# A softmax constant moved from the score products into ScalarE's exponentials, and the first chunk's output projection moved into the last attention group

## The reference, cut to what matters

```python
x = x + attention(layernorm(x))        # x: 2 batches x 1024 rows x 256
x = x + ffn(layernorm(x))
# attention: 32 query heads of width 8, 8 key heads
scores = einsum('bhqd,bhkd->bhqk', q, k) / sqrt(8)
amask = where((j >= i - 128) & (j < i), -1e10, 0)     # band below the diagonal
out = softmax(scores + amask) @ v ; out @ wo
# ffn: 2 shared experts on all rows, and 8 routed experts of which each row takes 2
# (sigmoid router), inner width 640, silu(gate) * up, then down
```

## Time and profile before

| | |
|---|---|
| median of 3 runs | 952.74 us (952.62 to 954.16) |
| the profiled execution | 952.9 us, span 951.2 us |
| mean granted clock of TensorE | 0.983 |
| busy share PE / DVE / ACT / POOL | 94% / 47% / 61% / 29% |
| chain that ended last | PE 78%, ACT 8%, DVE 6%, issue 5% |

### The profile page before, as it was taken

The page is one execution under the profiler, slowest core; times in us unless marked ns, Lnnn a source line. Parts: engine busy times, 40 slices in busy tenths (PEclk is TensorE's granted clock), DMA queues, the critical chain, the costliest instruction groups (busy, mean ns, idle before and its releaser), DMA issues.

```text
span 951.2 us, 24249 instructions
## 1 busy us (share of the span) xinstructions
PE 896.4 (94%) x8221; PEld 570.8 (60%) x8222; DVE 444.9 (47%) x761; ACT 583.4 (61%) x733; POOL 278.7 (29%) x422
## 2 busy tenths in 40 slices
PE   9959999999999999999988999999999999999994
PEld 6513333333333333333346888888887888888883
DVE  7724433444444334444456777656653433434332
ACT  4769999999999999999972423332222222222221
POOL 4403333233233333333330000000012545445442
PEclk9969999999999999999997999999999999999998
DMA  5433445555544455532202207100027864564521
GB/s 178 130 112 103 162 157 206 206 199 196 175 149 159 154 206 206 204 93 90 55 22 66 67 18 238 45 1 23 1 81 256 265 209 98 156 180 127 150 35 22
DMA packets 41951, 123.67 MB, mean 130 GB/s; under 512 B 7608, under 2 KB 22968, under 8 KB 35760
## 3 DMA queue, kind: packets, MB, share of 16 engines
q1 hardware_dynamic: 31152, 110.35, 34.0%
q0 software_dynamic: 7008, 9.70, 5.7%
q10 hardware_dynamic: 3744, 3.02, 1.0%
HBM read 74.03 MB, written 49.02 MB: 129 GB/s over the span
## 4 chain that ended last, share of the span: by engine, by line
PE 78%; ACT 8%; DVE 6%; issue 5%; SPq 1%; DMA 1%; DVEq 0%; POOLq 0%; POOL 0%; ACTq 0%
PE ps L1663 18%; PE ps L1811 14%; PE ps L1616 13%; PE ps L1765 11%; ACT arena L930 7%; PE ps L1830 7%; PE ps L1778 5%; DVE ps L1149 3%; PE ps L1557 2%; PE ps L1821 2%; PE ps L1716 1%; PE ps L1542 1%; PE ps L1792 1%; PE ps L1752 1%; PE ps L1734 1%
## 5 line engine op out<-in xcount | busy, mean ns | idle before, releaser
L930 ACT ACTIVATE arena<-ps 128x1024 f32<-128x1024 f32 x336 | 317.0, 1044 | 6.9 <-PE ps L1616 6.9
L1663 PE MATMUL ps<-arena 128*32 128x256 f32 x4096 | 265.1, 385 | 0.1
L759 POOL TENSOR_SCALAR_AFFINE_SELECT arena<-arena 128x512 f32<-128x512 f32 x240 | 150.0, 638 | 302.3 <-ACT arena L941 203.1
L1616 PE MATMUL ps<-arena 64*128 64x512 bf16 (+1 forms) x1280 | 184.5, 343 | 21.5 <-SPq L545 7.7
L1663 PEld LDWEIGHTS ps<-arena 128*32 128x32 f32 x4096 | 111.8, 109 | 103.1 <-issue 38.2
L1149 DVE COPY_PREDICATED ps<-keep,ps 128x512 f32<-128x512 int32 (+1 forms) x128 | 80.5, 629 | 172.1 <-PE ps L1616 172.1
L1616 PEld LDWEIGHTS ps<-arena 64*128 64x128 bf16 x1280 | 53.7, 94 | 175.4 <-ACT arena L930 82.2
L1811 PE MATMUL ps<-wr_all,x2T 128*128 x648 | 144.9, 364 | 5.7 <-issue 3.6
L1811 PEld LDWEIGHTS ps<-wr_all,x2T 128*128 128x128 f32 x648 | 105.6, 189 | 28.0 <-issue 13.7
L1765 PE MATMUL ps<-x2T,wr_all 128*128 128x512 f32 x480 | 118.8, 399 | 1.2 <-issue 1.2
L941 ACT ACTIVATE arena<-ps 128x1024 f32<-128x1024 f32 x112 | 114.2, 1034 | 8.0 <-DVE ps L1149 3.6
(11 more groups left out here) (187 smaller groups left out, 731.6 us busy)
## 6 DMA issues: line engine op xcount, KB each, us to landing
w_scr<-wr_all SPq DMA_DIRECT2D x24, 1280.0 KB, 7.0
wr_all<-w_scr SPq DMA_DIRECT2D x24, 1280.0 KB, 5.6
raw<-w_experts SPq DMA_DIRECT2D x24, 640.0 KB, 7.1
arena<-q_scr SPq DMA_DIRECT2D x64, 64.0 KB
o_scr<-arena SPq DMA_DIRECT2D x128, 32.0 KB, 1.6
arena<-o_scr SPq DMA_DIRECT2D x16, 256.0 KB, 3.9
raw<-w_shared SPq DMA_DIRECT2D x6, 640.0 KB, 4.2
q_scr<-parts SPq DMA_DIRECT2D x8, 384.0 KB, 2.8
```

The costliest lines, as they stand in the source:

```text
L759: nc.gpsimd.affine_select(out=dst, in_=src, compare_op=ALU.is_ge if own else ALU.is_gt, fill=0.0, base=0, pattern=[[0, REP], [-1 if own el ...
L930: nc.scalar.activation(prob[:, SLOT[unit(a, kt)], :, :].rearrange("p h q -> p (h q)"), score.rearrange("p b x -> p (b x)"), ACT.Exp, scale ...
L1616: return nc.tensor.matmul(ps[:, bank, :].rearrange("p (h q) -> p h q", h=2)[:, :, place * P:(place + tiles) * P], kst[r0:r0 + HALF, s, kt ...
L1663: last = nc.tensor.matmul(ps[32 * h:32 * h + 32, 6 + qc, a % 2 * QW:(a % 2 + 1) * QW], vst[:, s, kt, :], prob[:, SLOT[k], h, :], start=(no ...
```

## The change

The diff, cut to its core:

```diff
+XT_BANK = (4, 6, 6, 6)
+FIRST_O = (6, 2 * BUF[NEXP - 3])
```

On SP the credit for the zero rows goes from behind `load_stack(1, 1)` to the start, ahead of the loads of chunks 1 to 3, and the sums of chunk 0 are loaded between the stores of groups 10 and 11:

```diff
+            for s in range(2):
+                sp.sem_inc(st_in[s], 32)
             for c in range(1, NC):
                 load_rows(sp, c * TPC, (c + 1) * TPC, c)
...
             load_stack(1, 1)
-            for s in range(2):
-                sp.sem_inc(st_in[s], 32)
...
-            sp.wait_ge(o_stored[0], 16 * REP * KV + FIRST)
-            load_sums(0)
-            group_io(NG - 1, 1, False, False, False)
-            for c in range(1, NC):
+            for n in range(2 * LOOPED, NG - 1):
+                group_io(n, n % 2, n < SPLIT_PAIRS, n + 1 < NG - 1, n + 2 < NG)
+                if n == 2 * LOOPED:
+                    sp.wait_ge(o_stored[0], 16 * REP * KV + FIRST)
+                    load_sums(0)
+            store_acc(NG - 1, 0)
+            sp.wait_ge(o_stored[1], 16 * REP * KV + FIRST)
+            sp.wait_ge(c_proj, 2 + FIRST)
+            load_sums(1)
+            store_acc(NG - 1, 1)
+            for c in range(2, NC):
```

On POOL, in place of filling the rows of ones, both arrays are filled whole, `qst` with zeros, so that the row of ones in `kst` meets zeros:

```diff
-            pool.wait_ge(a_xn, 3)
-            pool.wait_ge(qst_zero, 1)
-            for half in range(2):
...
+            nc.gpsimd.memset(qst[:, :, :, :].bitcast(F32), 0.0).then_inc(const, 1)
+            nc.gpsimd.memset(kst[:, :, :].bitcast(F32), TWO_ONES).then_inc(const, 1)
```

On ACT (the exponential in all its three forms):

```diff
-                for k in range(KD):
+                for k in range(KD if c else 1):
                     nc.scalar.copy(x1T[:, c % 2, k, :], ps[:, k, :]).then_inc(a_xT, 1)
...
-            for s in range(2):
-                nc.scalar.copy(kst[HALF:HALF + 1, s, :], ps[HALF:HALF + 1, 7, 128:129].to_broadcast([1, L])) \
-                    .then_inc(shift_high, 1)
+            nc.scalar.copy(bound, ps[:, 7, 128:129]).then_inc(bound_ready, 1)
+            act.wait_ge(bound_ready, 1)
...
-                                             score.rearrange("p b x -> p (b x)"), ACT.Exp, scale=SCALE).then_inc(s_free, 1)
+                                             score.rearrange("p b x -> p (b x)"), ACT.Exp, bias=bound, scale=SCALE).then_inc(s_free, 1)
```

On DVE:

```diff
-            nc.vector.memset(qst[:, :, :, :].bitcast(F32), 0.0).then_inc(qst_zero, 1)
-            nc.vector.memset(kst[:, :, :].bitcast(F32), TWO_ONES).then_inc(const, 1)
...
+            row_stats(1, range(TPC))
+            dve.wait_ge(a_tp, 1)
+            nc.vector.tensor_copy(x1T[:, 0, 1, :], ps[:, 1, :]).then_inc(a_xT, 1)
...
-            dve.wait_ge(u_shift, 1)
-            for s in range(2):
-                nc.vector.tensor_copy(kst[0:1, s, :], ps[0:1, 7, 128:129].to_broadcast([1, L])).then_inc(shift_low, 1)
...
+            for n in range(2 * LOOPED, NG - 1):
+                i = n - 2 * LOOPED - 2
+                group(n, n % 2, n + 2 < NG, (lambda: invert(0, i)) if i >= 0 else (lambda: None))
...
+            def add_first(half):
+
+                dve.wait_ge(c_proj, half + 1 + FIRST)
+                for t in range(2 * half, 2 * half + 2):
+                    nc.vector.tensor_tensor(x_rows(0, t), x_rows(0, t), ps[:, FIRST_O[half], t % 2 * D:(t % 2 + 1) * D],
+                                            ALU.add) \
+                        .then_inc(c_added, 1)
+                for t in range(2 * half, 2 * half + 2):
+                    dve.wait_ge(c_added, t + 1)
+                    nc.vector.bn_stats(stats[:, t, :], x_rows(0, t)).then_inc(dve_step, 1)
```

On PE:

```diff
-            idle_turns(7, 52)
+            idle_turns(7, 30)
             transpose_x(0)
-            idle_turns(7, 8)
+            idle_turns(7, 4)
...
-            pe.wait_ge(shift_low, 1)
-            pe.wait_ge(shift_high, 1)
+            pe.wait_ge(const, N_CONST)
             for i in range(AHEAD):
                 scores(0, 0, 0, i)
+            pe.wait_ge(bound_ready, 1)
...
+            products_of(*last, LAST_MERGE + 2, False)
+            pe.wait_ge(c_oT, 1)
+            pe.wait_ge(merged, NG * NMERGE)
+            project(0, range(0, 2))
+            products_of(*last, LAST_MERGE + 3, False)
+            pe.wait_ge(s_free, NG * NEXP - 2 + BUFS)
+            project(0, range(2, 4))
```

More of the change, by code:

```diff
@@ L1193, in _ @@
                     group(it * 2 + s, s, True)
-            for n in range(2 * LOOPED, NG - 1):
-                group(n, n % 2, n + 2 < NG)
             def x_rows(c, t):
@@ L1666, in values, with products_of @@
                 last.then_inc(p_free, 1)
-            def turn_of(n, s, turn, t, before, after):
-                products, ended = TURNS[t]
-                for p in products:
+            def products_of(n, s, turn, t, after):
+                for p in TURNS[t][0]:
                     if not isinstance(p, int):
@@ L1677, in turn_of, with values_of @@
                         scores(n + 1, 1 - s, turn + s, ISSUE_NO[p - NEXP])
[L1678 removed]
+            def values_of(n, s, turn, t, before):
+                for v in TURNS[t][1]:
                     if len(v) == 2:
@@ L1682, in turn_of @@
                         values(n - 1, 1 - s, unit(*v[0:2]))
+            def turn_of(n, s, turn, t, before, after):
+                products_of(n, s, turn, t, after)
+                values_of(n, s, turn, t, before)
             def group(n, s, turn):
```

116 lines of the change are left out of this document (62 added, 54 removed).

## The result

The changed kernel is slower: 969.52 us median of 4 runs (966.74 to 970.98) against 953.34 of the kernel before, a ratio of 1.0166, 95% interval 1.0141 to 1.0191. The forecast was 973.9, within 934 to 983. Its profiled execution took 966.74 us with a span of 965.0; a later set of five runs gave 970.06 against 953.14 (1.0172, 1.0149 to 1.0194).

The account below looks back on a forecast made before the run. ACT's exponentials were taken to set the pace of stage B. From 952.9 us, minus 1.3, 6.7 and 8.8 of gains, plus 41.8 for the operand, minus 4.0 of idle time, came 973.9 us, range 934 to 983.

Parts of the forecast that it names:

- The operand: Stage B's exponentials on ACT: reading the bias from SBUF costs 0.09 us each, 464 x 0.09 = 41.8 us.
- DVE's 0.059: Lower price for an exponential's operand, from DVE's per-partition operand in us; it would give 959.5 us.
- the 0.12: Upper price for an exponential's operand, from the overlap of two neighbours in us; it would give 987.8 us.
- The idle time taken back: Stage B: ACT's idle 0.32 us a group shrinks, taking back 4.0 of 5.1 us.
- The first rival: Stage B's operand is free, hidden under the exponential before: 936.1 us; chance 0.33 with its variants.
- Stage A's start: First projections start sooner, at 11.0 us, through earlier statistics, fewer idle turns and shared copies: gain 1.3 us.
- A to B: Step from stage A to B: PE no longer waits for SP, first scores sooner by 6.7 us.
- B to C: Step from stage B to C: no late last group, no pause, higher clock: gain 8.8 us.
- The 0.67 of group 15: Stage B's last group ran 0.67 us late; moving DVE's inverts to groups 12 to 14 gains that.
- The cold start (third rival): Stage A: fewer turns leave PE's clock low, up to 5.5 us more; 979 us, chance 0.1 with priced operand.
- The tail (fourth): Stage B to C: DVE's chain outlasts the values, losing part of 8.8; at worst 980 us, chance 0.08.
- The marks: Signs to look for in the trace: exponential length and spacing, group time, first scores, projections, turned rows, clock.

Follow-up runs that it names:

- e1: The changed kernel with the bias operand taken out of its exponentials, the constant left out altogether: 940.74 us against 954.09.
- e6: e1 with stage A's start as in the kernel before (DVE fills the stacks, 52 and 8 idle turns, ACT copies both halves): 939.42 us.
- e12: The changed kernel run again, unaltered, for the spread of its runs: 970.06 us against 953.14.
- e4: e1 with SP's release of the zero rows put back behind the second stack's load: 947.86 us.
- e5: e1 with the tail put back as in the kernel before (first chunk's sums, inverts, projection, normalisation and turns at their old places): 949.57 us.
- e9: e1 with the band mask built only under the flag and wo and the router's weights issued later with their own semaphore: 938.37 us.
- e11: e1 with the softmax's constant back in a row of the key stack, as in the kernel before: 949.59 us.
- e10: e9 with the softmax's constant back in a row of the key stack, as in the kernel before: 949.04 us.

## Why the prediction held, and where it was off

The direction and the mechanism were right, and the measured 969.52 lies 4.4 us under the 973.9. That it lies so near is luck in part: the operand was put 9.0 us too dear and the gains 3.4 too large, and these errors, with a kernel before that ran 1.2 longer beside e1 than in its own profile, offset each other.

**The operand, forecast 41.8 - 4.0 = 37.8, measured 28.8.** The price of 0.09 us was mis-sized: 0.076 in spacing, 464 x 0.076 = 35.3, or 34.7 with the half-width ones at their 0.04. It came nearest from ACT's own rows (0.079, "about that again") and I went above it, towards the overlap. DVE's 0.059, the floor of my range, was too low and the 0.12 too high. The idle time taken back was mis-sized too: 34.7 - 28.8 = 5.9 by the medians, 34.7 - 26.0 = 8.7 by the traces of stage B, in place of 4.0, since an exponential that starts after a wait is counted busy for its whole 1.044, of which in an unbroken run 0.12 lie under its neighbour. By starts the slack is larger than the 0.32 us that are not busy: 28 x 0.920 + 0.53 = 26.29 of a group's 27.06, 0.77, of which 28.76 - (28 x 0.996 + 0.57) = 0.30 is left in the changed kernel. The first rival, a free operand, fell at once: 0.076 is above its 0.045.

**The rest, forecast -16.8, measured 940.74 - 954.09 = -13.4.**

*Stage A's start:* forecast -1.3, measured about +0.8 by the traces (0.6 gained, 1.43 lost) and +1.3 by the medians (e6). The first step was short: 11.54 for 11.0, since DVE's copy stands behind chunk 1's statistics, which themselves wait for their rows; in e12 they land later still and it is 12.30. The 30 turns ended at 7.2 and not at 6.5, which cost nothing, as the normed rows came later. The gain then met a collision of DVE with POOL, which the trace of before shows only on POOL, as the order there was the other way round: DVE's step starts at 33.77 and keeps 0.69, POOL's select at 33.79 takes 2.32. The sentence "POOL takes over both fills ... its next steps waited for chunk 3 anyway" counted POOL as free because nobody waits for it; that it slows DVE was in no row I read.

*A to B:* forecast -6.7. By the traces 57.49 - 51.40 = 6.1 in the changed kernel, or 8.32 - 1.55 = 6.8 from the last product of stage A's start; put back alone it is worth 6.6 by the trace and 7.1 by the medians (e4). The assumed 1.0 for PE's branch was 1.17.

*B to C:* forecast -8.8, measured -8.7 by the traces (20.54 - 11.81) and -8.8 by the runs (e5, with some of the clock around stage D's start in it). The parts were less good than the sum. The pause of 4.83 went and the turned rows rose in clock, as forecast. Twelve products took 3.41 where 2.75 were forecast, and the router's sixteen, which were not in the sum, gave 0.4 back (1.85 for 2.28). The 0.67 of group 15 is not to be seen: from its half-width exponential to its last it takes 20.57 in e1 and 20.38 before.

*Not in the sum:* in e1 the ten looped groups take 1.0 us more together than in the kernel before (272.4 against 271.5), and the changed kernel and e4 to e9 show the same pattern, a second group 0.4 longer and then every other one 0.1; e11, with the constant in the stacks, does not. Why is open. With the traces of e1 and of before the places add up: -6.5 to the first scores, +1.0 in stage B, -8.5 from B to C, +0.4 behind, 13.6 in all.

The cold start (third rival) did not come: twelve projections took 5.53 us with 30 turns ahead as with 52. The tail (fourth) did hide.

**The marks.** Exponentials forecast at 1.13 us with 1.01 of spacing, seen at 1.19 (mean) and 0.996; a group of 29.3, seen 28.76; first scores at 49.5, seen 51.40, and projections at 11.0, seen 11.54; turned rows right behind the last values at clock 1.00, as seen.

## What to carry over

On an engine that sets the pace, count the operands of its instructions: a [128,1] bias or scale that is the same on all partitions is cheaper as a constant in the instruction, or folded into a matmul that is done anyway, than read from SBUF by each: reading it 464 times cost 26 us of stage B here, its place in the stacks under 1 us of waits (the collision of e10 and e11 left aside). Price such a thing by the spacing of starts in an unbroken run, and measure idle time over all repetitions and not in one window. Before a difference of a microsecond is put down to an edit, look how far the same place moves between two executions of one kernel. And an engine that nobody waits for can still slow its neighbour: a fill or mask moved to POOL has to be laid against what DVE does in the same microseconds.

## What the runs showed of the hardware

- A per-partition operand of an ACTIVATE over 128x1024 from PSUM costs 0.076 us of spacing for the first and 0.093 for the second (0.920, 0.996, 1.089), while the mean length in the records grows by 148 and 293 ns (1044, 1192, 1485). Length alone would have given nearly twice the price for the first and over three times for the second.
- POOL's select from SBUF over 1920 columns held a DVE operation with two inputs in SBUF for 1.6 us (2.28 in place of 0.69), or was itself held for 0.54 (2.33 in place of 1.79), by which of the two started first.
- POOL's fill of a single partition's row, 1x2048, two of them in 3.69 us, held DVE's four normalisations of 128x256 for 2.9 us (4.26 in place of 1.38; 4.73 in e10), though they touch one partition. Each takes about as long as POOL's fill of 128x2048, 1.80 us.
- A stall of PE of 2.75 us in stage A was followed by products at a lower clock, 8.07 us in place of 5.56, so that it cost about twice its length (3.06 us in e10, followed by 6.91); one of 1.47 us was not.
- The granted clock falls in some executions of one kernel and not in others while PE is busy nearly throughout (0.86 and 1.00 from 680 to 700 us, PE busy 18.34 us of 20 in both), and from the 24 products of chunk 0 to the end the kernel then takes 442 to 444 us (e5, e9, e11, e12) in place of 438 to 440.
- The first projections start at 11.54 us in one execution of the changed kernel and at 12.30 in another, as chunk 1's rows land (DVE's statistics on them start at 9.28 and 10.04).
